# Two chained cross attentions: weight preparation moved to GpSimd and ScalarE, row sums from three matmuls instead of four

## What is computed

```python
# attention 0
q = x @ Wq + bq;  k = ctx @ Wk + bk;  v = ctx @ Wv + bv
w = softmax(q @ k.T / sqrt(512), axis=1)          # over the rows t of x
y = w @ v + x
n = (y - mean(y)) * rsqrt(var(y) + 1e-6) * gamma + beta
# attention 1
Q = n @ Wq1 + bq1;  K = ctx @ Wk1 + bk1;  V = ctx @ Wv1 + bv1
out = n + (softmax(Q @ K.T / sqrt(512), axis=-1) @ V) @ Wo1 + bo1
```

## Time and profile before

| | |
|---|---|
| median of 3 runs | 675.12 us (673.11 to 677.44) |
| the profiled execution's own time | 677.24 us |
| span of its trace | 675.2 us |
| mean granted TensorE clock, share of full speed | 0.992 |
| HBM read and written | 56.57 MB and 16.78 MB |

### The profile page before, as it was taken

The page is one execution under the profiler, slowest core; times in us unless marked ns, Lnnn a source line. Parts: engine busy times, 40 slices in busy tenths (PEclk is TensorE's granted clock), DMA queues, the critical chain, the costliest instruction groups (busy, mean ns, idle before and its releaser), DMA issues.

```text
span 675.2 us, 11584 instructions
## 1 busy us (share of the span) xinstructions
PE 661.7 (98%) x3806; PEld 567.1 (84%) x3806; DVE 452.1 (67%) x1027; ACT 451.9 (67%) x1046; POOL 450.7 (67%) x327
## 2 busy tenths in 40 slices
PE   9989979999999999999999999999999999999997
PEld 7866968889888888988888888988888898888876
DVE  2594685767849575775858575785857577585754
ACT  3454747768677776767776776867777676777562
POOL 0562926939587685939677693958768593967462
PEclk9998979999999999999999999999999999999999
DMA  8913005134150504215060503315060421501002
GB/s 317 375 53 125 32 32 182 38 98 152 39 209 31 217 2 153 93 65 184 31 217 31 184 33 102 146 44 205 31 217 9 148 92 71 178 31 62 1 33 93
DMA packets 33376, 73.54 MB, mean 109 GB/s; under 512 B 1905, under 2 KB 10609, under 8 KB 31313
## 3 DMA queue, kind: packets, MB, share of 16 engines
q1 hardware_dynamic: 33360, 73.35, 30.4%
HBM read 56.57 MB, written 16.78 MB: 109 GB/s over the span
## 4 chain that ended last, share of the span: by engine, by line
PE 91%; DVE 4%; issue 2%; ACT 1%; POOL 1%; POOLq 0%; DVEq 0%; ACTq 0%
PE bank L389 81%; PE bank L396 7%; PE bank L405 1%; DVE n L881 1%; PE bank L441 1%; POOL x_even L1201 1%; PE bank L447 1%; DVE bv_rows L918 1%; PE bank L426 1%; ACT nT_hi L643 0%; DVE pt_lo L854 0%; POOL prod L1192 0%; DVE wqk_lo L862 0%; DVE w_lo L992 0%; ACT y_hi L641 0%
## 5 line engine op out<-in xcount | busy, mean ns | idle before, releaser
L852 DVE SCALAR_TENSOR_TENSOR y_lo<-bank,ccol,y_hi 128x512 fp32r<-128x512 f32 x64 | 46.3, 751 | 102.4 <-ACT y_hi L641 102.4
L1208 POOL TENSOR_TENSOR r<-r,beta_b 128x512 f32<-128x512 f32 x60 | 101.5, 1722 | 0.0
L1184 POOL TENSOR_TENSOR rstd<-var_eps,minus_half 128x2 f32<-128x2 f32 x32 | 22.8, 713 | 111.2 <-DVE var_eps L1023 111.2
L641 ACT ACTIVATE y_hi<-bank,ccol 128x512 fp32r<-128x512 f32 x64 | 44.1, 691 | 61.2 <-PE bank L389 61.0
L1192 POOL TENSOR_TENSOR prod<-n,u_b 128x512 f32<-128x512 f32 x64 | 81.6, 1297 | 3.1 <-ACT prod L750 3.1
L1201 POOL TENSOR_TENSOR r<-n,gamma_b 128x512 f32<-128x512 f32 x60 | 75.8, 1297 | 0.0
L1001 DVE SCALAR_TENSOR_TENSOR r<-bank,rinv,r 128x512 f32<-128x512 f32 x60 | 44.9, 749 | 21.2 <-PE bank L389 17.1
L886 DVE TENSOR_TENSOR xT_lo<-x_raw,xT_hi 128x1024 fp32r<-128x1024 f32 x32 | 48.5, 1521 | 15.2 <-ACT xT_hi L671 15.2
L389 PE MATMUL bank<-wv_hi,wc_hi 128*128 128x512 f32 x128 | 53.1, 415 | 4.5 <-DVE rs_rows L1110 4.1
L389 PE MATMUL bank<-wv_hi,wc_lo 128*128 128x512 f32 x128 | 51.5, 403 | 0.0
L389 PE MATMUL bank<-wv_lo,wc_hi 128*128 128x512 f32 x128 | 51.4, 401 | 0.0
(11 more groups left out here) (176 smaller groups left out, 2166.8 us busy)
## 6 DMA issues: line engine op xcount, KB each, us to landing
x_raw<-in_x_turned_dram SPq DMA_DIRECT2D x16, 1024.0 KB, 7.8
out_dram<-r SPq DMA_DIRECT2D x30, 512.0 KB, 3.0
x_even<-in_x_dram SPq DMA_DIRECT2D x8, 1024.0 KB, 5.9
e<-in_ctx_turned_dram SPq DMA_DIRECT2D x16, 512.0 KB, 3.3
ctxn<-in_ctx_dram SPq DMA_DIRECT2D x16, 512.0 KB, 4.8
x_odd<-in_x_dram SPq DMA_DIRECT2D x8, 1024.0 KB, 5.8
wqkT<-in_wqk_turned_dram SPq DMA_DIRECT2D x4, 384.0 KB, 4.8
wqkT<-in_wqk_turned_dram SPq DMA_DIRECT2D x1, 1536.0 KB, 15.4
```

Source lines behind the costliest of these rows:

```text
L641: i = act.activation(dst, at((name, k))[:], ACT.Identity, bias=bias)
L852: i = dve.scalar_tensor_tensor(dst, src, bias, high.bitcast(F32), ALU.add, ALU.subtract)
L1184: pool.tensor_tensor(rstd[:, q], var_eps[:, q], minus_half[:, q], ALU.pow).then_inc(rstd_ready, 1)
L1208: pool.tensor_tensor(r[:, j, :], r[:, j, :], beta_b[:], ALU.add).then_inc(resid_ready, 1)
```

## The change

1. `row_sums` makes three matmuls: the two high blocks, and one over `w_lo_sum`, the sum of the two low blocks. GpSimd adds them (`add_w_lo`) after VectorE has made the low weights (it waits for `emptied` of `s0` 1), in the place ahead of `add_beta`. The sum lies in the buffer of `pt_lo` 0, free at that time. `row_sums` waits for the new semaphore `w_lo_added`.
2. The order becomes `wc` 0, `wc` 1, `rs` on TensorE, ScalarE and VectorE, and the banks of `wc` 1 and `rs` change places.
3. In the first pair `cut_v0` moves from VectorE to GpSimd, bias rows first. The four dot products become four multiplications on GpSimd (`beta_products`) and four copies with an accumulated output on ScalarE, which then adds the bias per column (`bias_through_wq1`). GpSimd's order is now `cut_cT`, `cut_ctx`, `cut_v0`, `add_w_lo`, `beta_products`, `bv_wo`, `x_products`, `rstds`.
4. TensorE makes `wvo` 0, `wvo` 1, `bo1`; VectorE does the low parts of `wvo` before `finish_beta`; ScalarE waits for `bo1` filled before it goes on to the next pair.

```diff
-          + [("wc", 0), ("rs", 0), ("wc", 1)] + tiles("s1", 2) + [("pr", 0), ("pr", 1)] + tiles("pt", 2)
+          + [("wc", 0), ("wc", 1), ("rs", 0)] + tiles("s1", 2) + [("pr", 0), ("pr", 1)] + tiles("pt", 2)
...
+        w_lo_sum = PT[1][:, 0].rearrange("p m t -> p (m t)")
...
             def row_sums(it):
 
-                wait_emptied(pe, it, "s0", 1)
+                pe.wait_ge(w_lo_added, it.times(1, 1))
                 dst = begin(it, "rs")
-                end(product(dst[:], [(ones_r[:], w[:, :, mt, :]) for w in W for mt in range(RM)]), "rs")
+                end(product(dst[:], [(ones_r[:], W[0][:, :, mt, :]) for mt in range(RM)] + [(ones_r[:], w_lo_sum)]),
+                    "rs")
...
+            def bias_through_wq1():
+
+                for e in range(KD):
+                    act.wait_ge(beta_prod_ready, e + 1)
+                    act.activation(N[:, e, :], N[:, e, :], ACT.Copy, accum_out=betaq[:, e:e + 1])\
+                       .then_inc(betaq_ready, 1)
+                for e in range(KD):
+                    act.wait_ge(betaq_ready, e + 1)
+                    act.activation(bq1_full[:, e:e + 1], betaq[:, e:e + 1], ACT.Identity,
+                                   bias=bq_col[1][:, e:e + 1]).then_inc(bq1_ready, 1)
...
                 for c in range(KC):
                     round_bank(it, "wvo", c, WVO[0][:, c, :])
                 wait_emptied(act, it, "t1")
+                wait_filled(act, it, "bo1")
...
-                if begin_it:
-                    cut_v0(it)
                 if it.front:
                     normalise0(it)
-                if begin_it:
-                    beta_wq1(it)
...
+            def cut_v0():
+
+                low_rows = slice(BV_STEP, 2 * BV_STEP)
+                pool.wait_ge(cn_lo, 1)
+                pool.wait_ge(bv_hi, 1)
+                pool.tensor_tensor(bv_rows[low_rows], prod[0][low_rows], bv_rows[low_rows].bitcast(F32),
+                                   ALU.subtract).then_inc(bv_lo, 1)
+                pool.wait_ge(bv_lo, 1)
+                pool.wait_ge(wv0_hi, 1)
+                pool.tensor_tensor(WV0[1][:], wv0_sb[:], WV0[0][:].bitcast(F32), ALU.subtract).then_inc(wv0_ready, 1)
+
+            def beta_products():
+
+                pool.wait_ge(half_in_or_stored[1], 16)
+                pool.wait_ge(loaded["wqk1"], 16)
+                pool.wait_ge(r0_ready, J)
+                for e in range(KD):
+                    pool.tensor_tensor(N[:, e, :], wqkT1[:, e, :D], beta_b[:], ALU.mult).then_inc(beta_prod_ready, 1)
...
+            def add_w_lo(it):
+
+                wait_emptied(pool, it, "s0", 1)
+                pool.tensor_tensor(w_lo_sum.rearrange("p (b t) -> p b t", b=2), W[1][:, :, 0, :].bitcast(F32),
+                                   W[1][:, :, 1, :].bitcast(F32), ALU.add).then_inc(w_lo_added, 1)
...
                     row_products(it, (2, 3))
                     if not it.front:
                         scale_n(it)
+                    else:
+                        add_w_lo(it)
                     add_beta(it, range(J))
                 if begin_it:
+                    cut_v0()
+                    add_w_lo(it)
+                    beta_products()
                     bv_wo()
```

More of the change, by code:

```diff
@@ L55 @@
 PREP1B = tiles("u1", 1)
-PREP1C = [("t1", 0), ("wvo", 0), ("bo1", 0), ("wvo", 1)]
-PREP_BANKS = (2, 3, 6, 7, 4, 5) + (7, 3) + (0,) + (5, 4, 6, 3)
+PREP1C = [("t1", 0), ("wvo", 0), ("wvo", 1), ("bo1", 0)]
+PREP_BANKS = (2, 3, 6, 7, 4, 5) + (7, 3) + (0,) + (5, 4, 3, 6)
 ROUND = 7
@@ L471, in prepare1c @@
                                          for h in range(KD)]), "wvo", c)
[L472 to L475, removed]
+                pe.wait_ge(bvwo_ready, 3)
+                dst = begin(it, "bo1")
+                end(product(dst[:], [(ones_r[:].bitcast(F32), bv_wo_sb[:, 0, :])]), "bo1")
             def transpose_n(it):
@@ L600, in iteration @@
                     weigh0(it, 0)
+                    weigh0(it, 1)
                     row_sums(it)
-                    weigh0(it, 1)
                 if begin_it:
@@ L803, in iteration @@
                     round_bank(it, "wc", 0, halves(WC[0], 0))
+                    round_bank(it, "wc", 1, halves(WC[0], 1))
                     round_row_sums(it)
-                    round_bank(it, "wc", 1, halves(WC[0], 1))
                 if more and it.back:
@@ L810, in iteration @@
                     round_xT(it, 1, 1)
+                    bias_through_wq1()
                     sum_x_products(it, range(J))
@@ L843, in _ @@
         def _(dve):
-            counted = {"prep": 0, "dots": 0}
+            counted = {"prep": 0}
             def low(it, name, k, dst, high, bias=None, per=0, back=0):
@@ L875, in low_wqk1 @@
                                 [gscale[:, 2 * g + n:2 * g + n + 1] for n in range(2)])
[L877 to L881, removed]
             def cut_xT(it, h, ahead):
@@ L897, in first_row_sums @@
                 for j in range(J):
-                    dot(r0[:, j:j + 1], XN[it.parity][:, j, :], at(("u0", 0))[:]).then_inc(r0_ready, 1)
+                    dve.tensor_tensor_reduce(N[:, j], XN[it.parity][:, j, :], at(("u0", 0))[:], 1.0, 0.0, ALU.mult,
+                                             ALU.add, r0[:, j:j + 1]).then_inc(r0_ready, 1)
                 wait_filled(dve, it, "t0")
@@ L910, in add_beta_to_bo @@
                 dve.tensor_tensor(bo1_b[:], bo1_b[:], beta_b[:], ALU.add).then_inc(beta_added, 1)
[L912 to L927, removed]
-                dve.wait_ge(dots_ready, KD)
-                dve.tensor_tensor(bq1_full[:], betaq[:], bq_col[1], ALU.add).then_inc(bq1_ready, 1)
             def prepare1a(it):
@@ L1107, in iteration @@
                     low(it, "wc", 0, halves(WC[1], 0), halves(WC[0], 0), per=2)
+                    low(it, "wc", 1, halves(WC[1], 1), halves(WC[0], 1), per=2)
                     dve.wait_ge(hi["rs"], it.times(1, 1))
@@ L1111, in iteration @@
                                       ALU.subtract).then_inc(emptied[BANK["rs", 0]], 1)
-                    low(it, "wc", 1, halves(WC[1], 1), halves(WC[0], 1), per=2)
                 if more and it.back:
```

11 lines of the change are left out of this document (6 added, 5 removed).

## The result

| | before | after |
|---|---|---|
| median of 6 runs each | 674.43 us (670.68 to 678.42) | 709.12 us (698.54 to 717.63) |
| ratio | | 1.0428, interval 1.0358 to 1.0499 |
| the profiled execution's own time | 677.24 us | 717.57 us |
| span of its trace | 675.2 us | 715.8 us |
| mean granted TensorE clock | 0.992 | 0.968 |

The change made the kernel 4.3% slower; the forecast was 1.8% faster. The runs of the kernel after spread over 19 us, those before over 8; a differing number of lost pairs, in the sense of the next paragraphs, would do that, but only one run of each is profiled.

A forecast was written before the change was run, and what follows sets the result against it. TensorE, busy 661.7 of 675.2 us, was taken to bound the kernel. First pair 2.3, row sums 3.5 and second pair 6.6 sum to 12.4 us, off the median of 675.12 giving 662.7; whole range 659.5 to 673.

The forecast's parts named there:

- the sum: Whole kernel: gains of 2.3 + 3.5 + 6.6 = 12.4 us, giving 662.7 us.
- rival B: Steady pairs: VectorE's `xT_lo` is starved by GpSimd, 6.6 us lost in each of 14, giving 755; chance 0.07.
- Part 1: Row sums: three matmuls for four on TensorE, 15 x 0.23 = 3.5 us won, the new GpSimd addition costing nothing.
- Rival C: Row sums: GpSimd's addition takes 1.9 us or more, `rs` comes late, up to 5.5 us lost; chance 0.07.
- Part 2: First pair: moved work closes TensorE's gaps, 2.3 us won, one-column products starting at 49.3.
- Part 3: Second pair: VectorE's request comes 0.63 us into a GpSimd instruction and wins, so the 7.16 us `xT_lo` goes, minus 6.6.

The follow-up runs named there:

- add_only: The kernel before plus GpSimd's addition of the low halves ahead of `add_beta`, its result read by nobody; median 700.21 us (688.09 to 734.02).
- prep_only: The kernel before with only the change's preparation of the first pair, row sums and order as before; 675.26 us, ratio 0.9941.
- gap64: The changed kernel with a GpSimd memset of 64 elements between the addition of low halves and `add_beta`; 674.77 us, ratio 0.9928.
- b_gaps: The kernel before with a GpSimd memset of 8 elements ahead of each `add_beta`; 680.1 us, ratio 1.0043.
- a_yield3: The changed kernel, GpSimd waiting for the first `xT_lo` ahead of `add_beta` 0, the second ahead of `add_beta` 1; 667.6 us, ratio 0.9848.
- pad400: The changed kernel with a GpSimd product of 400 elements ahead of the addition of low halves; 731.36 us (712.55 to 763.39).

## Why the prediction was wrong

**The step that failed** is the wait of the first `xT_lo` in the steady pairs, which the sum took as one boundary, at no cost, by dismissing rival B. Six of thirteen pairs were passed over instead, for 52.2 us. The rival was described in full, with its place, but got 7% on one sentence: "the same instruction lengths at the same phases won in every pair from the third on". Thirteen pairs of one execution of another row were taken for a rule. The same text had a counterexample, the second pair before, and said of it that what lets GpSimd keep the port is "seen once and not understood". A cause that is not understood, on which a 9-us loss hangs in each of fourteen pairs, doesn't get 7% when the edit adds an instruction to just that row. `add_only` shows it: 0.93 wins and 0.92 loses in one run. The sign that the text gave for being wrong in kind, an `xT_lo` of over 3 us from the third pair on, is what came.

**The price of B** was 6.6 a pair, from the second pair of before. It measured 8.7. Six GpSimd instructions begin behind the request where four did (it came in the second `add_beta`, at 81.67, and now comes in the addition ahead of the first), while 0.4 us of the one under way is left where it was 1.1. That makes `xT_lo` 1.7 longer, 8.88 against 7.16, and `pr` 0 waits 6.2 where it waited 3.83; about 2.5 more are slow clock. The forecast of 755 assumed all fourteen; six of them came in the profiled run, at 717.6. That it "decides as soon as two or three pairs lose it" was right: 12 won, 52 lost.

**Part 1** was right. Three matmuls stand where four stood, and nothing waits for the sum of low halves:

```profile
157.24 0.63 PE L391 MATMUL bank<-w_hi,ones_r 128*128 128x512 f32 x2
157.71 0.40 PE L391 MATMUL bank<-pt_lo,ones_r 128*128 128x512 f32 x1
157.95 0.28 PE L391 MATMUL bank<-cT_even_hi,y_hi 128*128 128x256 f32 x1
```

The addition took 1.27 to 1.36 (taken: 1.30), and ended 0.6 ahead of the first of the three, in front of which TensorE would wait for it (156.62 against 157.24), as forecast. A pair without a loss takes 38.34 to 38.41, 0.2 less than 38.56; 0.23 was the forecast. Rival C is dead with that.

**Part 2** was right in size and place: 2.7 won against 2.3, no gap at the wait for the first weights, and `bq1_full` by 46.6 against 46:

```profile
34.86 1.27 POOL L1203 TENSOR_TENSOR pt_lo<-w_lo 128x512 fp32r<-128x512 f32 x1 [1.93 <-DVE w_lo L983]
...
45.78 0.84 ACT L705 ACTIVATE bq_full<-betaq,cols 128x1 f32<-128x1 f32 x4
...
50.70 0.95 PE L443 MATMUL bank<-bq_full,wqkT 128*128 128x1 f32 x8
```

`bv_wo` was ready at 49.4 (forecast 48 to 50) and made nothing late. That the one-column products start at 50.7 instead of 49.3 is the slower clock ahead of 30 us: in `prep_only`, where it was 1.00, they start at 49.27.

**Part 3** came out as forecast in this run (1.93 us, and 6.5 won), but for a reason that doesn't hold. The request was 0.45 into the first `add_beta`, not 0.63. It came 0.50 in when it was lost in `prep_only`, and 0.40 when it was lost in `gap64`. It was luck, and against worse odds than in the later pairs: in the 14 profiles of kernels without a wait, the second pair's first `xT_lo` was lost in 12 (all but the kernel after and `b_gaps`), the later ones in 52 of 182.

**The sum** of what the change does outside the contest is confirmed by `a_yield3`: its span is 665.6, but its `wqk1` product begins at 30.77, 2.3 later than before; without that it is 663.3, against 675.2 - 12.4 = 662.8 of the forecast.

The Trainium skill, SBUF — State Buffer, Summary: rules for kernel authors, says that when VectorE has two SBUF inputs while GpSimd reads SBUF, the second one to issue blocks until the first finishes. The requests served at the first boundary fit that, as the two of the pair at 117.84. The 6 to 10 us of the lost ones don't: the waiter is passed over by instructions that GpSimd starts after the request, up to seven in `pad400`. The measurement decides.

## What to carry to other kernels

When a trace shows one instruction of VectorE, with both inputs in SBUF, that takes several times its siblings' time and ends where a row of GpSimd ends, treat it as a lottery that each pair may enter, and price an added GpSimd instruction in that row with it, not with its own 1.3 us alone. Break GpSimd's row with a wait on the very VectorE instruction, ahead of the instruction that would collide, and look that the waiting engine has the time to spare; that was worth 6% here, and made a 4% loss a 1.5% gain. Most of the gain is freedom from losses; the change by itself, with the first wait in both kernels, is worth 3.4 us. An experiment that adds the suspected instruction alone, read by nobody, separates this from the rest of a change; it wants several runs, as `add_only` spread from 688 to 734.

## What the runs showed of the hardware

- VectorE's `xT_lo` of 1.22 us took up to 9.9 us, while GpSimd began seven instructions after the request. VectorE is busy 68% of the span, and yet each subtraction of 8.9 us cost the span 8.7.
- Once passed over at the first boundary or two, a request was passed over to the end of the row in nearly all cases; the exceptions, four in all, took 2.4 to 2.7 us.
- After an instruction of GpSimd that VectorE had held up, VectorE was let in at the next boundary 101 times out of 101. The second `xT_lo` of a pair was never lost, whatever preceded it.
- A memset that reads nothing takes 0.09 to 0.19 us of GpSimd, and VectorE mostly got in beside it (13 of 13 pairs with 64 elements, 12 of 13 with 8, in one profile each).
- The stages ahead of 30 us are nearly the same work in all these kernels, but the `wqk1` product began between 28.45 and 31.6 us, with a granted clock of 1.00 in the earliest and 0.83 from 20 to 30 us in the latest. A difference of 3 us between two single profiles can be that alone.
